# Layer 1's experts: the hidden rows turned by fp32 matmuls with the identity, on two column strips, in place of whole-array transposes

## The chip, the core and the metric

One core of a Trainium2 chip runs the kernel. The metric is the device time of one execution in microseconds, the median over several runs. TensorE (PE in the profile; its weight loads are PEld) multiplies, VectorE (DVE) and ScalarE (ACT) work on rows, GpSimd (POOL) issues the indirect transfers, SyncE (SP) the plain ones.

## The reference

Two layers over x (4 x 512 tokens of 512, fp32), each a mixer and a mixture of experts. Only layer 1's experts matter here:

```python
T = 2048; E, K = 32, 8; H = 512; I = 256
tkw, top_k_index = ...                         # 8 of 32 experts for each token, by sigmoid scores
xs = jnp.repeat(x, K, axis=0)[sort_idx]        # 16384 rows, sorted by expert
gate = jax.lax.ragged_dot(xs, w_gate, group_sizes)     # 512 -> 256
up = jax.lax.ragged_dot(xs, w_up, group_sizes)         # 512 -> 256
down = jax.lax.ragged_dot(jax.nn.silu(gate) * up, w_down, group_sizes)   # 256 -> 512
routed = (down[unsort].reshape(T, K, H) * tkw[..., None]).sum(axis=1)
shared = jax.nn.silu(x @ sw_gate) * (x @ sw_up) @ sw_down
return routed + shared
```

## The kernel before

The program runs stage after stage: layer 0's mixer, its router and shared expert, its experts, layer 1's attention (`attention_stage`), its router and shared expert, and last `expert_stage1`, layer 1's experts. All arithmetic is fp32.

The rows of all experts lie in slots, sorted by expert. `expert_stage1` takes them in 144 tiles (`NTILE1`) of 128 rows; a tile is two halves of 64 rows, and each half belongs to one expert, so the two halves can have different weights. The array of TensorE is therefore used as two column strips of 64 (`tile_position=(0, s * HALF)`, s = 0 or 1): strip s holds the 64 rows of half s as stationary weights and multiplies its own expert's matrix. Strip 0 reads the matrix from the ring of four experts (`wgu`, `wd`), strip 1 from a copy that ScalarE (`cgu`) and VectorE (`cd`) make for each tile.

For each tile t:

- ScalarE loads rows ahead, four tiles at a time; VectorE turns them in 32 x 32 blocks into `xsT` (`turned_rows`).
- `up(t)` (line 2092) multiplies: four steps over the 512 inputs, two strips, 8 instructions with 512 moving columns. Gate and up values stand side by side in `ps_g`.
- ScalarE takes silu of the gate half into `sg` (line 1921, `gate`), VectorE multiplies by the up half into `h` (line 2019, `product`): 128 rows of 256.
- `turn_hidden(t)` (line 2099, the place of the change) turns `h`: `h[:, q % 2, a:F1:NW]` takes every second column, so part a (0 or 1) has 128 of the 256 columns, and its transpose lands in `ps_h`. VectorE copies that to `hT` (line 2014, `turned_hidden`).
- `down(t)` (line 2111) multiplies: two steps, two strips, 4 instructions with 512 moving columns, into `ps_o`.
- ScalarE scales the result into `yo` (line 1928, `empty`; eight buffers), and GpSimd adds it to the output rows in DRAM by two indirect transfers, one for each half (line 1874, `scatter`). Where a half belongs to another expert than the one before, its transfer waits until the one before has landed.

TensorE's order is written out in its `a_round`: `expert_of(t)` (reads the expert's number), `turn_hidden(t - 1)`, `up(t)`, `down(t - 1)`. So the turning of a tile stands between the `down` of the tile before it and the `up` of the tile behind it, and its input `h` is made while that `down` runs. It waits for the semaphore "h"; `down` waits for "hT". The other engines' orders are fixed in the same way by their own `a_round` or loop, two tiles deep (`q % 2`) in `h`, `hT`, `xsT`, `cgu`, `cd` and the accumulators.

The attention stage has two helpers that the prediction reads. `turn_d` (line 2926) and `turn_max` (line 2915) turn small pieces by `pe.matmul` with the identity as the moving operand, on column strips:

```python
# turn_d, in each of 16 groups: 4 instructions, all on one strip of 64
i = pe.matmul(ps[half:half + ND, at, j * P:(j + 1) * P], sd[:, j, g, :], ident[:, :],
              start=True, stop=True, skip_group_check=True, tile_position=(0, half))
# turn_max, in each of 16 groups: for j in 4, for hh in 4 strips of 32
i = pe.matmul(ps[hh * HD:(hh + 1) * HD, at, j * P:(j + 1) * P],
              nm[:, (TB * G + j) % 8, hh:hh + 1].to_broadcast([P, HD]), ident[:, :], ...)
```

`turn_x` (line 2869), `turn_head` (2882) and, in layer 0's experts, `turn_rows` (1672) use `pe.transpose` on the whole array, line 1672 with a stride of four columns in its weights.

Of the kernel before, what the change touches and what calls it, by code (L numbers as in the profile page):

```python
# [21 lines left out]
P = 128  # L22
# [16 lines left out]
F1, FS1, K1 = 256, 512, 8  # L39
# [3 lines left out]
HALF = P // 2  # L43
# [29 lines left out]
def hold(eng, sem, value, held):  # L73

    eng.wait_ge(sem, value)
    eng.sem_inc(held, 1)
# [1702 lines left out]
def expert_stage1(nc, c, I, D, x, ends, W, out):  # L1779
# [3 lines left out]
    with ExitStack() as ctx:  # L1783
        pl = Pools(nc, ctx)
        ctx.callback(pl.clear)
        NW = F1 // P
# [14 lines left out]
        h = pl.sb("e1_h", [P, 2, F1])  # L1801
# [20 lines left out]
        ps_h = pl.ps("e1_psh", [P, 2, 512])  # L1822
# [8 lines left out]
        half = lambda s: slice(s * HALF, (s + 1) * HALF)  # L1831
# [8 lines left out]
        with nc.Block() as block:  # L1840

            @block.sync
            def _(sp):
                sp.dma_start(ids[0:1, :], D["expert"][0:2 * NTILE1, :].rearrange("n o -> o n")).then_inc(sem["ids"], 16)

                def announce(s, turn):
                    hold(sp, landed[s], 1 + 48 * (turn + (1 if s >= AHEAD else 0)), c["held"])
                    sp.sem_inc(sem["ready"], 1)

                def refill(e, q):  # L1850
                    last = sp.value_load(ends[0:1, bass.ds(e, 1)], min_val=0, max_val=NTILE1)
                    hold(sp, sem["down"], 1 + last, c["held"])
                    s = (q + RING - 1) % RING
                    expert_weights(sp, I, W, e + RING - 1, s, landed[s])

                for s in range(AHEAD):
                    announce(s, 0)
                with sp.Fori(0, E // RING - 1) as i:
                    for q in range(RING):
                        refill(i * RING + q, q)  # L1860
                        announce((q + AHEAD) % RING, i + (1 if q > 0 else 0))
                refill(E - RING, 0)
                announce(AHEAD, E // RING - 1)
# [215 lines left out]
            @block.tensor  # L2079
            def _(pe):  # L2080
                def expert_of(t):
                    e = pe.value_load(ids[0:1, bass.ds(2 * t, 1)], min_val=0, max_val=E - 1)
                    hold(pe, sem["ready"], 1 + e + 1, c["held"])
                    return e

                def up(t, q, e):
                    pe.wait_ge(sem["xsT"], 1 + t + 1)
                    pe.wait_ge(sem["cgu"], 1 + t + 1)
                    for k in range(KH):
                        for s in range(2):  # L2090
                            w = cgu[:, q % 2, k, :] if s else wgu[:, bass.ds(e % RING, 1), k, :]
                            j = pe.matmul(ps_g[half(s), q % 2, :], xsT[:, q % 2, k, half(s)], w, start=k == 0, stop=k == KH - 1,  # L2092
                                          tile_position=(0, s * HALF), skip_group_check=True)
                    j.then_inc(sem["gu"], 1)

                def turn_hidden(t, q):
                    pe.wait_ge(sem["h"], 1 + t + 1)
                    for a in range(NW):
                        j = pe.transpose(ps_h[:, q % 2, a * P:(a + 1) * P], h[:, q % 2, a:F1:NW], c["ident"][:, :])  # L2099
                    j.then_inc(sem["htr"], 1)  # L2100

                def down(t, q, first=False):
                    e = pe.value_load(ids[0:1, bass.ds(2 * t, 1)], min_val=0, max_val=E - 1)
                    pe.wait_ge(sem["hT"], 1 + t + 1)
                    pe.wait_ge(sem["cd"], 1 + t + 1)
                    if not first:
                        pe.wait_ge(sem["yo"], 1 + t - 1)
                    for a in range(NW):
                        for s in range(2):
                            w = cd[:, q % 2, a, :] if s else wd[:, bass.ds(e % RING, 1), a, :]  # L2110
                            j = pe.matmul(ps_o[half(s), q % 2, :], hT[:, q % 2, a, half(s)], w, start=a == 0, stop=a == NW - 1,  # L2111
                                          tile_position=(0, s * HALF), skip_group_check=True)
                    j.then_inc(sem["down"], 1)

                def a_round(i, first=False, last=False):
                    for q in range(LAST if last else RING):
                        t = i * RING + q
                        e = expert_of(t)
                        if not (first and q == 0):
                            turn_hidden(t - 1, q + RING - 1)  # L2120
                        up(t, q, e)
                        if not (first and q == 0):
                            down(t - 1, q + RING - 1, first and q == 1)

                pe.wait_ge(sem["ids"], 1 + 16)
                a_round(0, first=True)
                with pe.Fori(1, ROUNDS - 1) as i:
                    a_round(i)
                a_round(ROUNDS - 1, last=True)
                turn_hidden(NTILE1 - 1, LAST - 1)  # L2130
                down(NTILE1 - 1, LAST - 1)

# [1082 lines left out]
```

## Time and profile before

| | |
|---|---|
| median of 3 runs | 3014.07 us (3013.24 to 3017.05) |
| profiled execution | 3016.98 us |
| its span | 3015.3 us, mean granted clock 0.954 |
| TensorE busy, all stages | 2646.6 us, 88% |
| layer 1's experts | from about 2171 us to the end |

The span runs from the first to the last recorded instruction of the execution. A matmul's record begins when it begins to stream and ends when its last result is out, so that consecutive matmuls overlap in the records: a matmul of 512 columns has a record of 0.59 us and the next one starts 0.43 us behind it; one of 128 columns has 0.27. What a matmul costs in a stream is therefore the distance from start to start. A row of the trace in order of time can stand for several instructions ("x2"); its time is then from the first start to the last end.

### The profile page before, as it was taken

What the parts mean: (1) busy time and instruction counts of PE and PEld (TensorE: products, weight loads), DVE (VectorE), ACT (ScalarE), POOL (GpSimd) and SP (SyncE); (2) the same over time, 40 slices, a digit from 0 to 9 for tenths busy, and PEclk for the clock granted to TensorE, in tenths of its full rate; (3) what the DMA queues carried; (4) which work ended last, traced back from release to release, by engine and by line L of the source; (5) the groups of instructions that cost most, each with busy time, mean ns of one, the idle gap of its engine ahead of it and who ended that gap; (6) DMA issues with size and microseconds to landing.
All of it is one profiled execution on the core that took longest, in us unless ns stands there. A gap on an engine that the chain in (4) does not pass through costs nothing. (4 is left out here: it accounts for less than half of the span.)

```text
span 3015.3 us, 39565 instructions
## 1 busy us (share of the span) xinstructions
PE 2646.6 (88%) x10453; PEld 1059.1 (35%) x10454; DVE 1539.7 (51%) x2654; ACT 1032.4 (34%) x1305; POOL 1290.9 (43%) x933
## 2 busy tenths in 40 slices
PE   5888976699999987778899998897199999999998
PEld 2343432244444433333333333443033333333332
DVE  7999999531110033146656564721155555555553
ACT  4646554110000011023433342200155555555553
POOL 2777656223200031116564542156445555445554
PEclk8999999999999999889999999898599999999999
DMA  4333222310200299882077000345577776787764
GB/s 129 113 96 111 82 65 71 116 57 15 90 28 14 79 317 341 262 235 58 1 198 199 12 1 0 126 187 208 158 166 147 159 148 118 151 196 162 160 110 61
DMA packets 361886, 372.81 MB, mean 124 GB/s; under 512 B 85810, under 2 KB 268403, under 8 KB 361778
## 3 DMA queue, kind: packets, MB, share of 16 engines
q1 hardware_dynamic: 202210, 239.03, 25.3%
q0 software_dynamic: 45520, 93.26, 14.7%
q10 hardware_dynamic: 114048, 39.16, 5.8%
q8 instruction: 57, 0.93, 0.1%
q14 instruction: 51, 0.42, 0.0%
HBM read 231.96 MB, written 152.14 MB: 127 GB/s over the span
## 5 line engine op out<-in xcount | busy, mean ns | idle before, releaser
L1874 POOL DMA_INDIRECT out_x<-e_yo,e_dest x288 | 416.1, 1445 | 435.3 <-DMA out_x<-e_yo,e_dest 314.6
L2092 PE MATMUL e_psg<-e_wgu,e_xsT 128*64 x1152 | 527.9, 601 | 81.7 <-ACT e_cgu L1947 81.7
L2092 PE MATMUL e_psg<-e_cgu,e_xsT 128*64 128x512 f32 x1152 | 527.9, 602 | 0.0
L287 POOL TENSOR_TENSOR hc<-hs,bcst 128x1024 f32<-128x1024 f32 x128 | 300.7, 2350 | 179.2 <-DVE ps_b L507 171.7
L1947 ACT ACTIVATE e_cgu<-e_wgu 128x2048 f32 x144 | 275.2, 1912 | 132.1 <-issue 130.0
L632 PE MATMUL ps_y<-hc,ident 128*128 128x512 f32 x512 | 241.2, 609 | 89.7 <-POOL hc L287 89.4
L513 DVE TENSOR_TENSOR_SCAN hs<-dA,ps_b 128x1024 f32<-128x1024 f32 x128 | 292.7, 2286 | 8.1 <-ACT dA L417 3.9
L2111 PE MATMUL e_pso<-e_wd,e_hT 128*64 x576 | 270.7, 592 | 0.7 <-DVE e_hT L2014 0.7
L2111 PE MATMUL e_pso<-e_cd,e_hT 128*64 128x512 f32 x576 | 270.7, 593 | 0.0
L2092 PEld LDWEIGHTS e_psg<-e_wgu,e_xsT 128*64 128x64 f32 x1152 | 146.7, 137 | 348.3 <-issue 331.0
L1237 PE MATMUL r_ps_t<-r_wd,r_h 128*128 128x512 f32 x480 | 210.8, 600 | 11.1 <-issue 6.0
L917 ACT ACTIVATE r_sg<-r_ps_g 128x512 f32<-128x512 f32 x60 | 35.8, 597 | 525.1 <-PE r_ps_g L1218 525.0
L984 DVE TENSOR_TENSOR r_h<-r_ps_u,r_sg 128x512 f32<-128x512 f32 x60 | 41.4, 691 | 319.7 <-PE r_ps_u L1218 308.8
L2019 DVE TENSOR_TENSOR e_h<-e_psg,e_sg 128x256 f32<-128x256 f32 x144 | 61.2, 425 | 273.9 <-ACT e_sg L1921 273.9
L417 ACT ACTIVATE dA<-dt,a_neg 128x511 f32<-128x511 f32 x256 | 165.2, 713 | 102.8 <-DVE hs L513 97.8
L2699 DVE TENSOR_REDUCE a_nm<-a_ps 128x2 f32<-128x992 f32 x128 | 146.1, 1185 | 88.7 <-PE a_ps L2943 88.3
L2461 ACT ACTIVATE a_pt<-a_ps 128x1024 f32<-128x1024 f32 (+1 forms) x128 | 126.1, 1022 | 185.7 <-PE a_ps L2960 124.9
L882 POOL DMA_INDIRECT slots_in<-r_xn,scat x128 | 126.1, 985 | 132.6 <-DMA slots_in<-r_xn,scat 54.5
L632 PEld LDWEIGHTS ps_y<-hc,ident 128*128 128x128 f32 x512 | 93.0, 191 | 232.4 <-POOL hc L287 138.9
L2009 DVE STREAM_TRANSPOSE e_xsT<-e_xs 128x512 f32<-128x512 f32 x144 | 172.1, 1195 | 4.1 <-DMA e_xs<-slots_in 4.1
L1928 ACT ACTIVATE e_yo<-e_pso,e_wrow 128x512 f32<-128x512 f32 x144 | 98.9, 687 | 206.7 <-PE e_pso L2111 200.9
L2027 DVE COPY e_cd<-e_wd 128x1024 f32 x144 | 102.7, 713 | 128.3 <-PE e_pso L2111 127.3
(427 smaller groups left out, 4158.7 us busy)
## 6 DMA issues: line engine op xcount, KB each, us to landing
slots_in<-zeros SPq DMA_DIRECT2D x144, 256.0 KB
e_xs<-slots_in ACTq DMA_DIRECT2D x144, 256.0 KB
bcst<-bc_rows SPq DMA_DIRECT2D x128, 256.0 KB, 4.2
e_wgu<-in_wg SPq DMA_DIRECT2D x32, 512.0 KB, 4.8
e_wgu<-in_wu SPq DMA_DIRECT2D x32, 512.0 KB, 5.9
e_wd<-in_wd SPq DMA_DIRECT2D x32, 512.0 KB, 7.7
e_w<-in_wg SPq DMA_DIRECT2D x11, 1408.0 KB, 16.8
e_w<-in_wu SPq DMA_DIRECT2D x11, 1408.0 KB, 17.9
```

The source lines that it names most:

```text
L287: pool.tensor_tensor(hc[:, it % 2, half(h), :], hs[:, it % 2, half(h), :], bc(bcst[:, q, 1, :], 1, HB), ALU.mult).then_inc(sem["hc"], 1)
L417: i = act.activation(dA[:, it % 2, t, 1:], dt[:, b % 2, t, 1:], ACT.Exp, scale=a_neg[:, n, t:t + 1])
L513: dve.tensor_tensor_scan(hs[:, it % 2, half(h), :].rearrange(flat), dA[:, it % 2, half(h), :].rearrange(flat), ps_b[:, :, :].rearrange(fla ...
L632: i = pe.matmul(ps_y[:, t, :], c["ident"][:, :], hc[:, it % 2, t, :], start=False, stop=False, skip_group_check=True)
L882: pool.indirect_dma_start(slots[:, :], bass.IndirectOffsetOnAxis(scat[:, t, k:k + 1], 0), xn[:, t, 0:XU], None, bounds_check=nslot - 1, oo ...
L1237: i = pe.matmul(ps_t[:, j % 2, :], h[:, f, j * P:(j + 1) * P], wd[:, f, :], start=f == 0, stop=f == FC - 1)
L1874: pool.indirect_dma_start(out[:, :], bass.IndirectOffsetOnAxis(dest[:, q, s:s + 1], 0), yo[half(s), q, :], None, bounds_check=T + 2 * P - ...
L1947: act.activation(cgu[:, q % 2, :, :], wgu[:, bass.ds(e % RING, 1), :, :].rearrange("p o k n -> p (o k) n"), ACT.Copy).then_inc(sem["cgu"], 1)
L2009: dve.transpose(xsT[:, q % 2, :, :].rearrange("p k (s j) -> p k s j", j=DQ), xs[:, q // RING % 2, part, :].rearrange("p s (i k) -> p k s i ...
L2092: j = pe.matmul(ps_g[half(s), q % 2, :], xsT[:, q % 2, k, half(s)], w, start=k == 0, stop=k == KH - 1, tile_position=(0, s * HALF), skip_g ...
L2111: j = pe.matmul(ps_o[half(s), q % 2, :], hT[:, q % 2, a, half(s)], w, start=a == 0, stop=a == NW - 1, tile_position=(0, s * HALF), skip_gr ...
L2699: dve.tensor_reduce(nm[:, i % 8, 2 * z:2 * z + 2], ps[:, at:at + 2, 0:S2], AX_X, ALU.max, negate=True)\
```

## The change

`turn_hidden` takes the part of `h` apart into its two halves of 64 columns and multiplies each with the identity, by a plain fp32 matmul on the column strip of its number, in place of one transpose through the whole array. The result stands in the same place of `ps_h`. Waits, semaphores and buffers stay.

```diff
                 def turn_hidden(t, q):
                     pe.wait_ge(sem["h"], 1 + t + 1)
                     for a in range(NW):
-                        j = pe.transpose(ps_h[:, q % 2, a * P:(a + 1) * P], h[:, q % 2, a:F1:NW], c["ident"][:, :])
+                        for s in range(2):
+                            w = h[:, q % 2, s * HALF * NW + a:(s + 1) * HALF * NW:NW]
+                            j = pe.matmul(ps_h[half(s), q % 2, a * P:(a + 1) * P], w, c["ident"][:, :], start=True, stop=True,
+                                          tile_position=(0, s * HALF), skip_group_check=True)
                     j.then_inc(sem["htr"], 1)
```

TensorE's program in the middle of the stage, before: `expert_of` (line 2082), the turning, the first two steps of `up`. "ISA" rows are register instructions; 64x512 is 64 weight columns by 512 moving ones.

```order
L2082 TENSOR_LOAD e_ids
L2082 ISA x2
L75 REGISTER_ALU
L2099 MATMUL e_psh<-ident,e_h 128x128 x2
L2092 ISA
L2092 MATMUL e_psg<-e_wgu,e_xsT 64x512
L2092 MATMUL e_psg<-e_cgu,e_xsT 64x512
```

The same place in the changed kernel:

```order
L2082 TENSOR_LOAD e_ids
L2082 ISA x2
L75 REGISTER_ALU
L2101 MATMUL e_psh<-ident,e_h 64x128 x4
L2092 ISA
L2092 MATMUL e_psg<-e_wgu,e_xsT 64x512
L2092 MATMUL e_psg<-e_cgu,e_xsT 64x512
```

Two instructions over the whole array have become four over half of it, in the shape of their neighbours; nothing has moved.

At the end of the stage, in the changed kernel, the last turning stands between two `down`s (line 2111 of before is line 2114 here, 2103 is 2106):

```order
L2114 ISA
L2114 MATMUL e_pso<-e_wd,e_hT 64x512
L2114 MATMUL e_pso<-e_cd,e_hT 64x512
L2101 MATMUL e_psh<-ident,e_h 64x128 x4
L2106 TENSOR_LOAD e_ids
L2106 ISA x2
L2114 ISA
L2114 MATMUL e_pso<-e_wd,e_hT 64x512
L2114 MATMUL e_pso<-e_cd,e_hT 64x512
```

Here too only the turning differs from before.

## Rows read from the trace of the kernel before

**Rows 1.** The page: span, busy time, the chain's engines and lines.

```profile
span 3015.3 us, 39565 instructions
PE 2646.6 (88%) x10453; PEld 1059.1 (35%) x10454; DVE 1539.7 (51%) x2654; ACT 1032.4 (34%) x1305; POOL 1290.9 (43%) x933
...
PE 27%; ACTq 0%; DMA 0%; ACT 0%; issue 0%; POOL 0%; POOLq 0%; DVE 0%
PE e_psg L2092 17%; PE e_pso L2111 8%; PE e_psh L2099 2%; ACTq L1933 0%; DMA out_x<-e_yo,e_dest 0%; ACTq L1938 0%; ACT e_cgu L1947 0%; ACTq L1940 0%; POOL out_x L1874 0%; ACTq L1945 0%; ACT e_yo L1928 0%; POOLq L1891 0%; POOLq L1902 0%; DVE
```

**Rows 2.** One window: busy us of each engine, clock, DMA share, GB/s.

```profile
2600.00:2900.00 300.00, 300.00 (x1364) 101.93 (x1362) 155.68 (x417) 155.91 (x158) 152.24 (x105) 1.00 0.76 166
```

**Rows 3.** The chain in order of time: start us, us, group.

```profile
2896.11 3.58 PE e_psg L2092 x16
...
2993.58 3.58 PE e_psg L2092 x16
```

**Rows 4.** TensorE in order of time through one tile.

```profile
2849.22 0.59 PE L2111 MATMUL e_pso<-e_wd,e_hT 128*64 x1
...
2849.75 0.50 PE L2099 MATMUL e_psh<-ident,e_h 128*128 128x128 f32 x2
2850.18 0.64 PE L2092 MATMUL e_psg<-e_wgu,e_xsT 128*64 x1
...
2850.66 0.59 PE L2092 MATMUL e_psg<-e_wgu,e_xsT 128*64 x1
...
2851.09 0.59 PE L2092 MATMUL e_psg<-e_wgu,e_xsT 128*64 x1
...
2853.23 0.59 PE L2092 MATMUL e_psg<-e_wgu,e_xsT 128*64 x1
```

**Rows 5.** VectorE in order of time, same tile.

```profile
2848.56 0.42 DVE L2019 TENSOR_TENSOR e_h<-e_psg,e_sg 128x256 f32<-128x256 f32 x1 [1.77 <-ACT e_sg L1921]
...
2852.09 0.41 DVE L2014 COPY e_hT<-e_psh 128x256 f32<-128x256 f32 x1
```

**Rows 6.** Weight loads in order of time, same turning.

```profile
2849.74 0.31 PEld L2099 LDWEIGHTS e_psh<-ident,e_h 128*128 128x128 f32 x2 [0.81 <-DVE e_h L2019]
```

**Rows 7.** TensorE in order of time, attention: whole-array shapes in a row.

```profile
1378.99 1.45 PE L2850 MATMUL a_ps<-r_xnT,a_ctxT 128*128 128x512 f32 x3
1380.28 0.60 PE L2869 MATMUL a_ps<-ident,a_xn 128*128 128x128 f32 x4
```

**Rows 8.** TensorE in order of time, attention: matmuls on column strips.

```profile
1340.18 1.08 PE L2915 MATMUL a_ps<-ident,a_nm 128*32 128x128 f32 x32
...
1382.85 1.09 PE L2926 MATMUL a_ps<-ident,a_sd 128*64 128x128 f32 x8 [1.97 <-DVE a_hd L2592]
1383.87 0.64 PE L2976 MATMUL a_ps<-a_acc,a_one 128*32 128x512 f32 x4
```

**Rows 9.** Line 2099's weight loads: ns min/median/max.

```profile
L2099 PEld LDWEIGHTS e_psh<-ident,e_h x288: 193/205/217, 2178.9 to 2998.9; 128*128 128x128 f32 x144
```

**Rows 10.** Weight loads of lines 2926, 2915 and 2882, same columns.

```profile
L2926 PEld LDWEIGHTS a_ps<-ident,a_sd x128: 132/137/138, 1382.8 to 1853.4; 128*64 128x64 f32 x128
...
L2915 PEld LDWEIGHTS a_ps<-ident,a_nm x512: 104/110/178, 1340.2 to 1831.9; 128*32 128x32 f32 x171
...
L2882 PEld LDWEIGHTS a_ps<-ident,a_hd x112: 137/141/232, 1308.3 to 1710.8; 128*128 128x128 f32 x112
```

**Rows 11.** TensorE in order of time, layer 0's experts.

```profile
1102.52 0.75 PE L1672 MATMUL e_psx<-ident,r_wgu 128*128 128x128 f32 x4
```

**Rows 12.** GpSimd in order of time, two stretches.

```profile
2220.86 1.42 POOL L1874 DMA_INDIRECT out_x<-e_yo,e_dest  x1 [0.30 <-issue]
...
2385.25 1.55 POOL L1874 DMA_INDIRECT out_x<-e_yo,e_dest  x1 [0.47 <-DMA out_x<-e_yo,e_dest]
...
2389.11 1.43 POOL L1874 DMA_INDIRECT out_x<-e_yo,e_dest  x1 [0.46 <-DMA out_x<-e_yo,e_dest]
```

**Rows 13.** ScalarE in order of time, at tile 3.

```profile
2202.00 0.69 ACT L1928 ACTIVATE e_yo<-e_pso,e_wrow 128x512 f32<-128x512 f32 x1 [1.33 <-PE e_pso L2111]
```

## The prediction, made before the changed kernel ran

> **What bounds the kernel now.** I read the page first, then the windows of the last stage, the chain that ended last, and the order of time inside one tile. TensorE is busy 88% of the whole span, and the chain that ended last is 27% of the span on TensorE, all of it in lines 2092, 2111 and 2099, the lines of layer 1's experts [rows 1]. In a window of that stage the matmul engine is busy for all of its 300 us, at a granted clock of 1.00 (2.4 GHz); VectorE, ScalarE and GpSimd are busy for about half of it [rows 2]. The chain repeats exactly: from 2896.11 to 2993.58 lie 17 tiles, 5.73 us each [rows 3]. So a nanosecond that leaves TensorE's own sequence leaves each tile, until something else is late.
>
> Inside a tile [rows 4] the step between two pairs of matmuls (one per column strip) is 0.43 us: 2850.66 to 2851.09. Around the turning the steps are different. From the last pair of `down` (2849.22) to the first transpose (2849.75) it is 0.53, from there to `up`'s first pair (2850.18) 0.43 for both transposes, and from `up`'s first pair to its second (2850.66) 0.48. These four instants span 1.44 us. The input h is not what the turning waits for: h is ready at 2848.56 + 0.42 = 2848.98 [rows 5], 0.77 us ahead of it. What it waits for is the array: the weights of the transposes are loaded only at 2849.74 [rows 6], 0.09 us after the last pair has streamed its 0.43. The same gap stands behind `up`.
>
> The trace shows when that gap appears. Whole-array transposes behind whole-array matmuls have none: three matmuls from 1378.99, spaced (1.45 - 0.59)/2 = 0.43, put the last at 1379.85, and the transposes start at 1380.28, again 0.43 later, though the code has a wait ahead of them too [rows 7]. Where a 64-column group is followed by a 32-column one it is there: the last of the 64-column matmuls starts at 1382.85 + 1.09 - 0.27 = 1383.67, the next shape at 1383.87, 0.20 behind a matmul that streams 0.11 [rows 8]. So a change of the array's shape costs about 0.09 us and a slower first pair, another 0.05 in `up` (0.48 against 0.43).
>
> **What the change does, and its price.** It removes two whole-array transposes per tile and adds four fp32 matmuls, two on each strip. Their shape on the array is that of `down` and `up`, so both changes of shape go away: 0.09 + 0.09 + 0.05 = 0.23 us per tile removed. What the turning itself costs must be counted in array passes. The two transposes leave 288 records in 144 tiles, one each [rows 9]. An fp32 matmul leaves two: line 2926 issues 4 in each of 16 groups, 64 in all, and has 128 records, line 2915 issues 256 and has 512 [rows 10]; `up` issues 8 per tile and shows as x16 [rows 3]. So the new turning has 8 records, four per strip, in 4 rows of two strips.
>
> What does a row cost? Line 2915 is nearly the same thing already: identity as the moving operand, 128 columns, weights from data on column strips, strips issued in turn. Its 32 records on four strips take 1.08 us, eight rows: (1.08 - 0.27)/7 = 0.116 with a slower first step. Line 2926, on one strip, takes (1.09 - 0.27)/7 = 0.117, also with a slower first step [rows 8]. In a running stream the step follows the columns: 0.43 x 128/512 = 0.107, and the four transposes of 1380.28 take (0.60 - 0.27)/3 = 0.11 each [rows 7]. I take 0.109, since here the weights can be loaded one row ahead, and keep 0.117 as the upper bound. The sum: last pair of `down` to turning 0.429, four rows 0.436, `up`'s first pair to its second 0.429, together 1.294 against 1.44, so **0.146 us per tile** saved. The array work grows (0.436 against two whole-array steps of 0.11) and the shape changes saved are worth more.
>
> 142 tiles have a turning between a `down` and an `up`. Tile 0's turning waits for h, with an idle array before it, and behind the last one comes no `up` but the last `down`, which needs the copied result. I count both at nothing: the first row in an idle array has its own slower step [rows 8], and the end of the turning lies where it did (0.53 + 0.22 before, 0.43 + 0.33 after, from `down`'s last pair to its last start). 142 x 0.146 = 20.7 us.
>
> **What is late next.** Removing 0.146 per tile must not uncover another wait. The new loads are wanted when `down`'s last pair starts (2849.22), and h is there 0.24 us before (2848.98) [rows 4, 5]; that distance does not change, since both follow from the end of `up`. If the load slipped, the turning would still have 0.67 us until its matmul. e_hT, copied by DVE, is ready at 2852.09 + 0.41 = 2852.50 and first wanted for a load at 2853.23 [rows 4, 5]: 0.73 left, 0.58 afterwards. GpSimd's two scatters per tile are slower than they look: released by landings they take 3.85 us per tile when it is behind (2385.25 to 2389.11) [rows 12], against 5.59 available. Its worst lag is in the beginning, where tile 3's e_yo is written at 2202.69 [rows 13] and scattered at 2220.86 [rows 12], 18 us. There are eight buffers, 45 us of cover; a faster TensorE adds under 0.15 per tile to a lag that ends every few tiles. The DMA engines' share is 0.76 [rows 2]; 2.6% more is no bound. All of these I cost at nothing.
>
> **One unknown price: the stride.** The weights of the turning are every second column of h, and no fp32 matmul of this trace loads strided weights; transposes do. Contiguous ones load in 0.141 (line 2882), those of 2099 (stride 2) in 0.205 [rows 9, 10]; line 1672's (stride 4) are spaced (0.75 - 0.28 - 0.22)/2 = 0.12 [rows 11], when the first step is taken as 2099's, 0.50 - 0.28 = 0.22 [rows 4]. Below: a load of 64 columns takes 0.137 contiguous (line 2926) [rows 10], and fewer columns may hide the stride wholly, price 0. Above: rows go at the 0.12 of the 128-column strided transposes, +0.011 x 4 = 0.044 per tile, 6.2 us. I take 0, nearer to the 64-column row, and keep 6.2 for the range.
>
> One rule speaks against the change. The rows first: a whole-array transpose of 128 columns steps by 0.11, one fp32 matmul record of 128 columns by 0.11 too, and there are two records [rows 7, 8, 10], so a matmul is twice a transpose and two strips side by side repay that. The Trainium skill (TensorE: Matmul & The Clock Gate, Terms) says that the transpose mode is 4x faster for FP32. By that an fp32 matmul would take four passes, the turning 0.87 instead of 0.436, and the time would be about 3055. The records here say two.
>
> **Rivals.** (1) *The strips take turns.* If two loads per row, or identity read by both strips, cannot run side by side at 128 columns, the eight records go one after another at 0.109: 0.872 per tile, 0.29 more than now (0.436 more than in my sum, less 0.146). The kernel is slower: 142 x 0.29 = 41 us, 3055. It decides from a row of 0.146 us on, where gain and price are equal. For it: matmuls as short as these on just two strips stand nowhere in the trace. Against: line 2915's 32 records take 1.08 us; one after another they would take 3.5 [rows 8]. A matmul that takes four passes gives the same time (the rule above gives it, too). 8% together.
> (2) *The stride holds the rows* at 0.12: 3014.1 - 14.5 = 2999.5. 18%. A load slowed further, to a row of 0.14 to 0.15, would eat the gain: 3010 to 3016. 5%.
> (3) *The loads come late.* If h's semaphore reaches the queue only after `down`'s last pair has begun, part of the 0.09 stays, as a wait for the load: 0.05 to 0.09 per tile, 7 to 13 us, 3000 to 3006. For it: only 0.24 us between h and the wanted load. 7%.
> (4) *The gain is taken back by the scatters*, as lag beyond eight buffers: no change. Against: 18 us of lag, 45 of cover. 2%.
> (5) The forecast: rows of 0.109 and no gap. 60%.
>
> **The numbers.** The profiled execution took 3016.98 (span 3015.3); the median of three is 3014.07, the highest 3017.05, so the profiled one is among the slow of the three by 3 us, and I set the difference against the median: 3014.1 - 20.7 = 2993.4. Alone, the forecast lies between 2991 and 2996 (rows of 0.109 to 0.112 and 1 us of spread). The range reaches to the stride's and the late load's cases: 2990 to 3005. A change of 0.2%, 6 us, is about what a measurement can tell from none. Faster than 3008: 60 + 18 + 7 = 85%, and 1% of the 5; within: the rest of the 5 and the 2, 6%; slower: 8%.
>
> **What would show it.** In the profile after: the turning has 1152 records, on 64 columns of the array, instead of 288; its first record starts 0.43 behind `down`'s last pair, rows step by 0.11, `up` starts 0.11 behind the last of them and its second pair 0.43 behind its first; the chain's tile is 5.59 us. TensorE is still busy all the time. A row of 0.12 shows the stride, partners of a row 0.11 apart instead of 0.01 show strips in turn, a first record 0.5 behind `down` shows a late load, and idle time of TensorE on e_hT or e_yo shows that another engine has become the bound. The prediction is wrong if the tile stays over 5.65 us.

## The result: 2993.7 us, 0.8% faster, and the profile after

| | before | changed |
|---|---|---|
| median of 5 runs | 3017.05 us (3013.24 to 3020.09) | 2993.71 us (2988.94 to 2999.56) |
| profiled execution | 3016.98 us | 2994.60 us |
| its span | 3015.3 us | 2992.8 us |
| ratio, with 95% interval | | 0.992 (0.9903 to 0.9937) |

The prediction was 2993.4, between 2990 and 3005. The difference of the medians is 23.3 us where 20.7 were forecast; each kernel's runs spread over 7 to 11 us, so the 2.6 between them say nothing by themselves.

The page of the changed kernel answers to [rows 1]. The trace has 862 more matmul records, and TensorE is busy 24.5 us less:

```profile
span 2992.8 us, 41291 instructions
PE 2622.1 (88%) x11315; PEld 1086.1 (36%) x11318; DVE 1535.3 (51%) x2654; ACT 1032.8 (35%) x1305; POOL 1294.2 (43%) x933
...
PE 27%; ACTq 0%; DMA 0%; ACT 0%; issue 0%; POOL 0%; POOLq 0%; DVE 0%
```

The window of [rows 2], same columns:

```profile
2600.00:2900.00 300.00, 300.00 (x1722) 116.15 (x1720) 157.94 (x431) 159.98 (x162) 156.54 (x108) 1.00 0.77 167
```

TensorE still has no idle time in it, at the same clock, with 1722 records where there were 1364. Nothing else has become the bound.

The chain in order of time, as in [rows 3]:

```profile
2831.43 3.43 PE e_psg L2092 x16
2837.01 3.43 PE e_psg L2092 x16
...
2971.09 3.43 PE e_psg L2092 x16
2974.53 1.74 PE e_pso L2114 x8
```

From 2831.43 to 2971.09 lie 25 tiles, 5.586 us each, against 5.733 before. The chain counts a group from the end of the record ahead of it to its own last end, so the row of `up` holds what lies between the turning's last record and `up`: 3.43 where it was 3.58, and the 0.15 between them is the whole difference of a tile.

Where the difference arises is seen in TensorE's order of time, the place of [rows 4] in another tile:

```profile
2829.96 0.59 PE L2114 MATMUL e_pso<-e_wd,e_hT 128*64 x1
...
2830.39 0.59 PE L2114 MATMUL e_pso<-e_wd,e_hT 128*64 x1
...
2830.82 0.61 PE L2101 MATMUL e_psh<-ident,e_h 128*64 128x128 f32 x8
2831.26 0.59 PE L2092 MATMUL e_psg<-e_wgu,e_xsT 128*64 x1
...
2831.69 0.59 PE L2092 MATMUL e_psg<-e_wgu,e_xsT 128*64 x1
```

The steps are 0.43, 0.44 and 0.43 (2830.39, 2830.82, 2831.26, 2831.69): 1.30 in place of 1.44. The turning starts exactly one step behind `down`'s last pair, `up` starts one row of 0.11 behind the turning's last row, and `up`'s second pair comes after a plain 0.43. The eight records of the turning are one row of the view, and take 0.61: (0.61 - 0.27)/3 = 0.11 for each of the three steps between four rows of two strips.

All records of that line, with the shortest, median and longest in ns:

```profile
L2101 PEld LDWEIGHTS e_psh<-ident,e_h x1152: 136/138/138, 2177.1 to 2976.3; 128*64 128x64 f32 x192
L2101 PE MATMUL e_psh<-ident,e_h x1152: 272/273/327, 2177.1 to 2976.4; 128*64 128x128 f32 x192
```

1152 records are 8 in each of 144 tiles: two for each fp32 matmul. A load of every second column of 64 takes 0.138 us, what the contiguous one of [rows 10] takes.

The weight loads in order of time, and VectorE's, show what the turning waits for now; they answer to [rows 5, 6]:

```profile
2830.39 0.14 PEld L2101 LDWEIGHTS e_psh<-ident,e_h 128*64 128x64 f32 x2 [0.29 <-DVE e_h L2019]
2830.82 0.36 PEld L2101 LDWEIGHTS e_psh<-ident,e_h 128*64 128x64 f32 x6 [0.28 <-issue]
```

```profile
2829.74 0.42 DVE L2019 TENSOR_TENSOR e_h<-e_psg,e_sg 128x256 f32<-128x256 f32 x1 [1.65 <-issue]
...
2833.24 0.38 DVE L2014 COPY e_hT<-e_psh 128x256 f32<-128x256 f32 x1
```

The first load of the turning begins at 2830.39, with `down`'s last pair, a whole step before its matmul; before, it began at the same instant as its transpose. h is ready at 2829.74 + 0.42 = 2830.16, 0.23 ahead of the load. e_hT is ready at 2833.62.

**The sum of the spans.** 142 tiles by 0.1467 (5.7333 less 5.5867, the periods over the whole stage) make 20.8 of the 22.5 us between the spans of the two profiled executions. From the first turning to the last the trace has 819.87 us before and 798.95 in the changed kernel, and the same 798.95, within 0.01, in each of the five other kernels below with this tile (e2, e6 to e9) and in the changed kernel's second profile (e12), while their spans go from 2992.5 to 2998.9. So what the stage gains is fixed, and what their times differ by lies outside those 144 turnings. The rest of the 22.5 lies before the first whole tile: the chain has `up` of tile 0 starting at 2170.53, against 2171.73 before, and the distance from there to tile 1 was shorter by 0.56. Both vary in the kernels below without any edit of theirs there (stage starts from 2168.6 to 2176.7, first distances from 7.0 to 8.5), so they are no part of the change.

### The profile page after: what moved, and what is told of

It is laid out like the page before. It is cut to its first block and busy times, and to the rows that moved or that the text cites. A ratio compares the mean times of both kernels' runs of the same rounds, so it can differ in the third digit from the quotient of the medians.

```text
span 2992.8 us, 41291 instructions
## 1 busy us (share of the span) xinstructions
PE 2622.1 (88%) x11315; PEld 1086.1 (36%) x11318; DVE 1535.3 (51%) x2654; ACT 1032.8 (35%) x1305; POOL 1294.2 (43%) x933
## 5 line engine op out<-in xcount | busy, mean ns | idle before, releaser
L2092 PE MATMUL e_psg<-e_wgu,e_xsT 128*64 x1152 | 519.9, 594 | 83.0 <-ACT e_cgu L1947 83.0
L2092 PE MATMUL e_psg<-e_cgu,e_xsT 128*64 128x512 f32 x1152 | 519.9, 594 | 0.0
L2092 PEld LDWEIGHTS e_psg<-e_wgu,e_xsT 128*64 128x64 f32 x1152 | 154.2, 137 | 332.0 <-issue 332.0
```

## The experiments

Twelve kernels ran in three groups, each beside runs of the kernel before on its own chip: e1, e2, e3 and e6 (median of before 3019.49), e4, e5, e7 and e8 (3015.27), e9 to e12 (3014.86). In the expectations, theory A is what I held more likely, in most of them the account behind the prediction; the other letters are rivals. The period of a tile is from the chain of each; it repeats within 0.002 us in all of them but e10.

**e1: fp32 matmuls without the strips.** Before, with line 2099 as

```diff
-                        j = pe.transpose(ps_h[:, q % 2, a * P:(a + 1) * P], h[:, q % 2, a:F1:NW], c["ident"][:, :])
+                        j = pe.matmul(ps_h[:, q % 2, a * P:(a + 1) * P], h[:, q % 2, a:F1:NW], c["ident"][:, :], start=True, stop=True)
```

> The kernel before with two plain fp32 matmuls over the whole array in the turning, in place of the two transposes: one part of the change alone (matmul for transpose), without the column strips. Theory A (the gain is the two changes of the array's shape that go away, less the doubled passes): both changes of shape stay, and the turning has 4 records instead of 2, two more rows of 0.11 us; a tile takes 5.73 + 0.22 = 5.95 us, the kernel about 3045 us, 1% slower than before. Rival B (the gain comes from plain matmuls whose loads are fetched ahead, whatever their shape): 5.59 us per tile and about 2993 us.

Measured: tile 5.968, 3049.27 us (median of 4), ratio 1.0101 (1.0082 to 1.012). TensorE in order of time:

```profile
2840.00 0.59 PE L2111 MATMUL e_pso<-e_wd,e_hT 128*64 x1
...
2840.53 0.74 PE L2099 MATMUL e_psh<-ident,e_h 128*128 128x128 f32 x4
2841.20 0.64 PE L2092 MATMUL e_psg<-e_wgu,e_xsT 128*64 x1
...
2841.68 0.59 PE L2092 MATMUL e_psg<-e_wgu,e_xsT 128*64 x1
```

The 0.53 ahead of the turning and the 0.48 behind `up`'s first pair are back, as in before. Half the edit, the operation without the strips, makes the kernel slower than before by 1%. The gain is not in the fp32 matmul.

**e2: the stride taken out of the changed kernel.** VectorE writes h so that each part's columns stand side by side:

```diff
-                    dve.tensor_tensor(h[:, q % 2, :], ps_g[:, q % 2, F1:], sg[:, q % 2, :], ALU.mult).then_inc(sem["h"], 1)
+                    dve.tensor_tensor(h[:, q % 2, :].rearrange("p (a i) -> p a i", a=NW),
+                                      ps_g[:, q % 2, F1:].rearrange("p (i a) -> p a i", a=NW),
+                                      sg[:, q % 2, :].rearrange("p (i a) -> p a i", a=NW), ALU.mult).then_inc(sem["h"], 1)
...
-                            w = h[:, q % 2, s * HALF * NW + a:(s + 1) * HALF * NW:NW]
+                            w = h[:, q % 2, a * P + s * HALF:a * P + (s + 1) * HALF]
```

> The changed kernel, with h written by VectorE in the order in which the turning reads it, so that its weights are contiguous. Theory A (a stride in 64 columns of fp32 weights costs nothing, since the load is hidden behind the row before): tile 5.59 us, loads 0.138 us, time as the changed kernel, 2993 us. Rival C (rows of strided weights are a little slower than they could be): rows fall below the present step, tile 5.55 us, 2988 us. VectorE's product reads with a stride now; if it takes over 0.15 us longer, the turning's first load comes late, and the tile grows by what is over.

Measured: tile 5.586, 2996.95 us (6), ratio 0.9931 (0.9914 to 0.9948). The stride of 64-column weights costs nothing in the tile, the value that the prediction chose for its unknown.

**e3: the stride taken out of the kernel before.** The same product on VectorE, and whole-array transposes of contiguous columns:

```diff
-                        j = pe.transpose(ps_h[:, q % 2, a * P:(a + 1) * P], h[:, q % 2, a:F1:NW], c["ident"][:, :])
+                        j = pe.transpose(ps_h[:, q % 2, a * P:(a + 1) * P], h[:, q % 2, a * P:(a + 1) * P], c["ident"][:, :])
```

> The kernel before, whole-array transposes, with h laid out so that their weights are contiguous. Theory A: the loads take 0.14 us instead of 0.205, and the step from the first transpose to the second, 0.22 us now because the second load is not done, falls to 0.16; the changes of shape stay. Tile 5.67 us, kernel about 3006 us, between the two kernels. Rival D (most of the gain of the change was the strided load of the transposes, not the shape): tile about 5.60 us, 2994 us.

Measured: tile 5.669, 3007.32 us (6), ratio 0.9961 (0.9946 to 0.9975). Its weight loads take 0.140 where before's took 0.205 [rows 9]:

```profile
L2101 PEld LDWEIGHTS e_psh<-ident,e_h x288: 138/140/142, 2178.7 to 2989.6; 128*128 128x128 f32 x144
```

TensorE in order of time:

```profile
2841.58 0.59 PE L2113 MATMUL e_pso<-e_wd,e_hT 128*64 x1
...
2842.11 0.44 PE L2101 MATMUL e_psh<-ident,e_h 128*128 128x128 f32 x2
2842.48 0.64 PE L2094 MATMUL e_psg<-e_wgu,e_xsT 128*64 x1
...
2842.96 0.59 PE L2094 MATMUL e_psg<-e_wgu,e_xsT 128*64 x1
```

The 0.53 and the 0.48 stay; only the middle is shorter, 0.37 from the turning to `up` in place of 0.43. So 0.064 of the 0.147 was to be had by the layout alone, with the transposes kept; the other 0.083 is what the strips add. Of the 0.064, 0.056 is in the step from the first transpose to the second (0.221 before, 0.165 here). The records show what it is. Line 2099 in the kernel before, and the same line here:

```profile
L2099 PE MATMUL e_psh<-ident,e_h x288: 280/332/385, 2178.9 to 2999.0; 128*128 128x128 f32 x144
```

```profile
L2101 PE MATMUL e_psh<-ident,e_h x288: 272/300/330, 2178.7 to 2989.7; 128*128 128x128 f32 x144
```

The longest record of each is the first transpose's. Its load was not done ahead: load and matmul records start within 0.003 of each other, so such a record begins before the matmul can stream, and it is longer than the usual 0.273 by the load less 0.082. A load of 0.194 gives 0.385 (before, and e1), 0.186 gives 0.377 (e11), 0.138 gives 0.328 (here, and e4); `up`'s first pair behind the turning, loads of 0.133, has 0.643 in place of 0.592. This holds within 0.003 us in every tile of these kernels. So the slower first row behind a change of shape is the part of a weight load that shows, and a stride makes that load longer.

**e11: e1 without its stride.** The product of e2 and e3, and

```diff
-                        j = pe.transpose(ps_h[:, q % 2, a * P:(a + 1) * P], h[:, q % 2, a:F1:NW], c["ident"][:, :])
+                        j = pe.matmul(ps_h[:, q % 2, a * P:(a + 1) * P], h[:, q % 2, a * P:(a + 1) * P], c["ident"][:, :], start=True, stop=True)
```

> The kernel before with plain fp32 matmuls over the whole array and contiguous weights. Beside the strided one of the first call (tile 5.968 us) it gives the price of the stride for 128 columns of plain fp32 weights, beside the changed kernel (5.587) the price of the two changes of shape without any stride. Theory A: 4 rows of 0.109, two changes of shape of 0.094, and a slower first step of 0.05 behind each: tile 5.587 + 0.30 = 5.88 us, 3036 us. Rival D (the stride is most of it): tile 5.75 us or less, 3017 us.

Measured: tile 5.942, 3046.07 us (4), ratio 1.0099 (1.0084 to 1.0114).

```profile
2843.53 0.59 PE L2113 MATMUL e_pso<-e_wd,e_hT 128*64 x1
...
2844.06 0.71 PE L2101 MATMUL e_psh<-ident,e_h 128*128 128x128 f32 x4
2844.70 0.64 PE L2094 MATMUL e_psg<-e_wgu,e_xsT 128*64 x1
...
2845.18 0.59 PE L2094 MATMUL e_psg<-e_wgu,e_xsT 128*64 x1
```

Four rows of 128 moving columns here, four rows there: between this kernel and the changed one the operation and the number of rows are the same, and the strips alone are worth 5.942 - 5.586 = 0.356 us per tile. It was expected at 5.88. The first row is what was mis-sized: it takes 0.21 to the second, not 0.16. Its load shows, and an fp32 matmul's load of 128 columns takes 0.190 here, a transpose's contiguous one 0.140 (e3).

**e4: one shape change put back.** The changed kernel with a whole-array transpose of the identity, into columns of `ps_h` that nobody reads, ahead of the turning:

```diff
+                    pe.transpose(ps_h[:, q % 2, NW * P:(NW + 1) * P], c["ident"][:, :], c["ident"][:, :])
                     for a in range(NW):
                         for s in range(2):
```

> The changed kernel with one more instruction at the head of each turning: a whole-array transpose of the identity into columns of the accumulator that nobody reads. It puts one pair of changes of shape back. Theory A: 0.109 for the row, 0.094 for each of the two changes of shape, 0.05 for the slower first row behind the second: 0.35 us per tile, tile 5.93 us, kernel 3043 us. Rival F (a change of shape is cheap, and the gap before the turning was the late start of strided loads of 128 columns): 0.11 to 0.16 per tile, tile 5.70 to 5.75 us, 3009 to 3016 us.

Measured: tile 6.000, 3057.67 us (4), ratio 1.0141 (1.0125 to 1.0157).

```profile
2840.40 0.59 PE L2115 MATMUL e_pso<-e_wd,e_hT 128*64 x1
...
2840.93 0.33 PE L2098 MATMUL e_psh<-ident 128*128 128x128 f32 x1
2841.19 0.66 PE L2102 MATMUL e_psh<-ident,e_h 128*64 128x128 f32 x8
2841.68 0.59 PE L2092 MATMUL e_psg<-e_wgu,e_xsT 128*64 x1
```

One transpose of 0.109 costs 0.413. Each of the two shape changes around it has the gap of 0.094 (2840.40 to 2840.93 is 0.53 for a pair that streams 0.43) and a first row whose record is 0.33 in place of 0.27, another 0.055: 0.109 + 2 x (0.094 + 0.055) = 0.407. (The gap is 0.101 counted from strip 0's last matmul and 0.094 from strip 1's, which starts 0.007 later; the 0.006 left of the 0.413 is that.) The expectation had counted the slower first row only once. A change of shape is 0.15 us, 0.094 of gap and 0.055 of a load that shows, and it is what the edit under study took away twice. The 0.055 by itself stands in e10, without a change of shape; what makes up the gap no run here takes apart.

**e5: the turning done twice.** The loop of the changed kernel runs over its two parts twice, with the same result:

```diff
-                    for a in range(NW):
+                    for a in [a for _ in range(2) for a in range(NW)]:
```

> The changed kernel with the turning's four matmuls issued twice (same result). Theory A (TensorE bounds every tile, and a row of two strips costs 0.109 us, or 0.107 as the columns say): 4 x 0.109 more per tile, tile 6.02 us, kernel 3055 us. Rival G (part of the turning is hidden behind something else that bounds the tile): less than 0.3 us per tile, under 3037 us.

Measured: tile 6.023, 3062.34 us (4), ratio 1.0162 (1.0144 to 1.018). The profiled span is 3054.4, 61.6 above the changed kernel's, where 142 x 0.436 are 61.9. The profiled execution is the shortest of the four (3056.1 to 3066.4); no trace shows what the others have more.

```profile
2844.96 1.04 PE L2101 MATMUL e_psh<-ident,e_h 128*64 128x128 f32 x16
2845.84 0.59 PE L2092 MATMUL e_psg<-e_wgu,e_xsT 128*64 x1
```

0.436 more per tile: four rows more, 0.109 each. Nothing hides them, and nothing else in the tile grows. This is the price of the work that the edit adds.

**e6: strip after strip.** The changed kernel with its two loops swapped, so that strip 0's two matmuls are issued before strip 1's:

```diff
-                    for a in range(NW):
-                        for s in range(2):
+                    for s in range(2):
+                        for a in range(NW):
```

> The changed kernel with the turning's four matmuls issued as strip 0, strip 0, strip 1, strip 1 in place of 0, 1, 0, 1; same work and shape. Theory A (two strips run side by side only where their matmuls are neighbours in the program, since matmuls start in order): six or seven rows in place of four, a turning of 0.65 to 0.76 us, tile 5.80 to 5.91 us, 3024 to 3040 us, the price that the rival of strips in turn had in the prediction. Rival E (TensorE pairs the strips whatever their order): tile 5.59 us, 2993 us.

Measured: tile 5.586, 2989.84 us (4), ratio 0.9901 (0.9883 to 0.9919). Theory A is wrong here, its rival right. With four runs, and the profiled one the longest at 3000.70, the lower median shows no gain: from the first turning to the last it takes the 798.95 of the changed kernel.

```profile
2842.02 0.59 PE L2114 MATMUL e_pso<-e_wd,e_hT 128*64 x1
2842.08 0.59 PE L2114 MATMUL e_pso<-e_cd,e_hT 128*64 128x512 f32 x1
2842.45 0.66 PE L2101 MATMUL e_psh<-ident,e_h 128*64 128x128 f32 x8
2842.88 0.59 PE L2092 MATMUL e_psg<-e_wgu,e_xsT 128*64 x1
2842.94 0.59 PE L2092 MATMUL e_psg<-e_cgu,e_xsT 128*64 128x512 f32 x1
```

The strips' partners start 0.06 apart in all matmuls of the stage (0.01 in the changed kernel), and each strip keeps its pace: 0.43 from 2842.02 to 2842.45 to 2842.88. Two strips work side by side even when their instructions do not alternate.

**e7: the same edit in layer 0's experts.** Both places there that turn rows with whole-array transposes, lines 1672 and 1695, were given strips in the same way; the second has contiguous weights:

```diff
-                        i = pe.transpose(ps_x[:, k * P:(k + 1) * P], row(t)[:, k:H:KH], ident[:, :])
+                        for s in range(2):
+                            i = pe.matmul(ps_x[half(s), k * P:(k + 1) * P], row(t)[:, s * CAP * KH + k:(s + 1) * CAP * KH:KH],
+                                          ident[:, :], start=True, stop=True, tile_position=(0, s * CAP), skip_group_check=True)
```

> The changed kernel with the same edit in layer 0's experts: their turn_rows (4 transposes) and turn_hidden (3) become fp32 matmuls on two column strips, in 16 tiles. There the DMA engines' share is 0.93 and TensorE is busy for 172 of 230 us, so theory A expects no difference: 16 tiles, 8 + 6 rows of 0.109 in place of 7 transposes and up to four changes of shape, within 3 us of 2993 us either way. Rival H (TensorE sets the pace there too, at least for the tiles whose weights have landed): the stage grows or shrinks by 0.2 to 0.4 us per tile, 3 to 6 us.

Measured: layer 1's tile 5.586, 3000.64 us (6, from 2995.87 to 3009.90), ratio 0.9957 (0.9941 to 0.9973). Layer 0's experts ran from 1060.8 to 1275.9, 215.1 us, against 211.1 in the changed kernel, 213.7 in before, and 209.5 to 214.9 in e4, e5 and e8, which don't touch them. No gain shows. Whether it costs some us stays open: its interval overlaps those of e8 (0.9943, same group) and of e2 (0.9931), but lies just above the changed kernel's two (up to 0.9937 and 0.994).

**e8 to e10: a later h.** The prediction's third rival was a load that comes late. e8 put VectorE's small operations of `addressed` ahead of the product:

```diff
-                        product(t, q)
                         addressed(t, q, i + 1)
+                        product(t, q)
```

> The changed kernel with VectorE's product behind its small operations on addresses (product and addressed swapped), which makes h ready about 0.55 us later: 0.3 us after the turning's first load is wanted and 0.1 us before its first matmul. It asks what a late load costs, the third rival of the prediction. Theory A (the load then overlaps the last pair of down only in part, and the first row streams as from an idle array): 0.02 to 0.10 us per tile, tile 5.61 to 5.69 us, 2996 to 3008 us. Rival I (a load that comes late is as dear as the change of shape was, or more): 0.15 us or more per tile, 3015 us or more.

Measured: tile 5.586, 2998.14 us (5), ratio 0.9943 (0.9924 to 0.9962). It does not answer its question: the small operations ran while VectorE waited for `sg` anyway (in one tile from 2847.94 to 2848.48, the product from 2850.16), and h was ready 0.23 ahead of the wanted load, as in the changed kernel. e9 and e10 have one and two idle products into a buffer of their own ahead of the real one (here e9, e10 has 2 for 1):

```diff
+                    dve.wait_ge(sem["late"], 1 + 1 * t)
+                    for v in range(1):
+                        dve.tensor_tensor(void[:, v, :], ps_g[:, q % 2, F1:], sg[:, q % 2, :], ALU.mult).then_inc(sem["late"], 1)
                     dve.tensor_tensor(h[:, q % 2, :], ps_g[:, q % 2, F1:], sg[:, q % 2, :], ALU.mult).then_inc(sem["h"], 1)
```

> The changed kernel with VectorE's product made once more into a buffer that nobody reads, ahead of the real one (0.42 us each): h is really ready later now, about 0.2 us after the turning's first load is wanted and 0.2 us before its first matmul can start. Theory A (a load that comes late but ends before the array is free costs nothing or the 0.05 us of a first row that was not loaded ahead): tile 5.59 to 5.64 us, 2994 to 3001 us. Rival I (a late load is as dear as a change of shape was): 0.15 us or more, tile 5.74 us, 3015 us.

Measured for e9: tile 5.586, 2994.76 us (4), ratio 0.9934 (0.992 to 0.9949). VectorE, the weight loads and TensorE of one tile:

```profile
2847.40 0.41 DVE L2023 TENSOR_TENSOR e_h<-e_psg,e_sg 128x256 f32<-128x256 f32 x1
```

```profile
2847.87 0.56 PEld L2105 LDWEIGHTS e_psh<-ident,e_h 128*64 128x64 f32 x8 [0.52 <-DVE e_h L2023]
```

```profile
2847.64 0.59 PE L2118 MATMUL e_pso<-e_wd,e_hT 128*64 x1
...
2848.07 0.61 PE L2105 MATMUL e_psh<-ident,e_h 128*64 128x128 f32 x8
2848.51 0.59 PE L2096 MATMUL e_psg<-e_wgu,e_xsT 128*64 x1
```

h is ready at 2847.81, and the load starts at 2847.87, 0.23 later than it would have (2847.64); in most tiles it is 0.15. The first matmul is still one step behind `down`'s last pair, at 2848.07. A load that is late but done before the array is free costs nothing.

> The same with two idle products ahead of the real one: h is ready about 0.2 us after the last pair of down has streamed. Theory A: TensorE waits those 0.2 us (0.23 with the semaphore) and 0.05 for the first row, 0.28 per tile, tile 5.87 us, 3034 us; VectorE's copy of the turned rows comes 0.84 us later too and is still in time. If that copy is late for down as well, another 0.1 to 0.3. Rival J (h has more slack than the trace seems to show): tile 5.59 us.

Measured for e10: tile 5.70 in most places and 5.87 in every eighth (5.82 the first time), where h comes 0.17 later still; 3013.38 us (10), ratio 1.0001 (0.9992 to 1.001). VectorE and TensorE:

```profile
2850.36 0.76 DVE L2022 TENSOR_TENSOR e_void<-e_psg,e_sg 128x256 f32<-128x256 f32 x2 [1.15 <-ACT e_sg L1922]
2851.03 0.42 DVE L2023 TENSOR_TENSOR e_h<-e_psg,e_sg 128x256 f32<-128x256 f32 x1
```

```profile
2851.01 0.59 PE L2118 MATMUL e_pso<-e_wd,e_hT 128*64 x1
...
2851.50 0.66 PE L2105 MATMUL e_psh<-ident,e_h 128*64 128x128 f32 x8
2851.99 0.59 PE L2096 MATMUL e_psg<-e_wgu,e_xsT 128*64 x1
```

h is ready at 2851.45, and the stream of `down`'s last pair ends at 2851.01 + 0.43 = 2851.44. The turning starts at 2851.50, 0.06 late, and takes 0.49 to `up` in place of 0.44, because its first load could not go ahead. Together that is 0.11 per tile. From the first turning to the last the kernel takes 18.8 us more than the changed one, most of the gain. The expectation had 5.87 for all tiles: products back to back start 0.34 apart, less than their 0.42 records, so h came 0.2 earlier than I had counted. The matmul starts 0.05 behind h here, and in the changed kernel 0.66 behind it, so the cover of h there is 0.61. Beyond it each nanosecond costs one (every eighth tile: 0.17 later, 0.17 longer), after a step of 0.05.

**e12: the changed kernel once more,** with no edit, beside e9 to e11.

> The changed kernel once more, beside the kernel before on this call's chip. Calls have differed by some microseconds (the kernel before had medians of 3015 to 3019 us). Theory A: ratio 0.9931, which is 20.8 us of 3015, inside the interval; the tile is 5.587 us again. If the median difference again exceeds 23 us, something outside the tiles of this stage has gained too.

Measured: tile 5.586, 2994.69 us (6), ratio 0.9927 (0.9915 to 0.994), against 3014.86 of before: 20.2 us.

## Why the prediction was right, and where it was loose

**TensorE's own sequence is the bound, and a nanosecond leaves each tile.** Right. Busy for all of the window after, and every kernel's time follows its tile: 142 x 0.1467 = 20.8 us against 20.2 (e12) and 23.3 (the first comparison).

**The array's shape changes are the price of the transposes.** Right; shown by e1 and e11 (same rows, no strips: +0.382 and, without the stride, +0.356 against the changed kernel), and from the other side by e4 (one whole-array transpose put back: +0.413). The price itself was put together wrongly: 0.23 removed and two rows of 0.109 added would save 0.01, not the 0.146 of the sum. The prediction took 0.09 + 0.09 + 0.05 = 0.23 out for the shape changes; e3 and e4 say 0.15 for each of two, 0.30, and another 0.064 for the strided weights behind one of them (e3). Of the missing 0.13, 0.11 was the slow 0.22 from the first to the second transpose, twice a row, which the prediction named in its part on the stride, as a first step, and did not count among what goes away. e3's expectation laid it to the second load; the records lay it to the first, which shows in a row's length whatever follows. The total did not suffer, since it was the difference of two measured stretches (1.44 less 1.294), and that is why the number is right although its parts are not: in full, 0.30 + 0.064 removed, two rows of 0.109 added, 0.146 saved.

**Two records for an fp32 matmul, four rows of 0.109.** Right: 1152 records, rows of 0.11; e5 adds exactly 0.436 for four more. The Trainium skill (TensorE: Matmul & The Clock Gate, Terms) has the transpose mode 4x faster for FP32. The records here say 2x: a transpose is one of 0.109, a matmul two.

**The strips work side by side.** Right, and more robust than the rival allowed: they do so even in e6's order.

**The stride costs nothing.** Right at 64 columns (e2). It does cost where 128 columns are loaded: 0.064 per tile for transposes (e3 against before), 0.026 for fp32 matmuls (e1 against e11). So the bound of 0.12 a row was drawn from a case of another width. (The prediction's sum for it, (0.75 - 0.28 - 0.22)/2, gives 0.125 by the rounded figures; by those of the trace it is the 0.12 that the prediction has.)

**The loads are in time.** Right, with the margin as read (0.23 to the wanted load). The rival priced a late load too high: it charged 0.05 to 0.09 as soon as h passed the time of the wanted load. In e9 the load is late by up to 0.23 and nothing is paid; e10, with h ready when the array is free, pays 0.11. The 0.67 that the prediction saw left for h is 0.61 by e10.

**Nothing else comes late.** Right. e_hT is ready 0.64 us ahead of `down`'s first load in the median tile (0.77 before) and 0.28 in the nearest but the last; a load that waits for it starts 0.19 behind it (most tiles of e10), so the rest is the real margin. TensorE waits for e_hT once, 0.7 us in the last tile, as it did before. Tile 3's scatter starts 16 us behind its e_yo, no later than before; the longest lag is that of tile 2's second scatter, 22 us before and 20 now, and the prediction had overlooked it.

**The first and last turning at nothing.** Not settled: the first distance was 0.56 shorter in the profiled pair, but varies by 1.5 us between kernels whose edits don't bear on it.

No kernel here beat the changed one. Those with the same tile (e2, e6 to e9) have medians from 2989.8 to 3000.6 us, and the same 798.95 us from the first turning to the last.

## What to carry to other kernels

Read a small operation between two big ones by the distances from start to start around it, not by its own record: here two transposes of 0.11 us each had 0.36 us of gaps and of loads that showed around them. Where the neighbours run on parts of the array, the same work in the neighbours' shape can pay for twice the rows; without the shape, it loses. And before replacing an operation over strided weights, try them contiguous: 0.064 of the 0.147 us needed no new operation. Not tried here, and so open: `pe.transpose` itself on the two strips. With one record each it would have two rows where the fp32 matmuls have four, if the array runs it so.

## What the runs showed of the hardware that I had not expected

- The two column strips run side by side in whatever order their instructions come: issued 0, 0, 1, 1 they stay 0.06 us apart, with the same tile of 5.586 (e6).
- A weight load may start 0.23 us late and cost nothing, since it lies under the stream of the pair before it; with h ready just as that stream ends, the turning is 0.06 late and its first row 0.05 slower (e9, e10).
- Where a load could not go ahead, its row is longer by the load less 0.082 us: loads of 0.133, 0.138, 0.186 and 0.194 give 0.051, 0.055, 0.104 and 0.112, within 0.003 in every tile (before, e1, e3, e4, e10, e11). With no change of shape (e10) this is all; a change of shape adds a gap of 0.094 before it.
- A load of 128 columns over the whole array depends on the operation and the stride: 0.140 contiguous and 0.205 strided for transposes, 0.190 and 0.196 for fp32 matmuls. With 64 columns it is 0.138 either way.
- Products of VectorE with records of 0.42 us start 0.34 apart when they follow each other.
